# Mixture-of-experts combine: weighted rows added into DRAM by accumulating scatters, instead of a gather and a weighted sum on VectorE

## The reference

```python
flat = rmsnorm(mamba_out + residual, ln_ff_w).reshape(T, D)      # T = 1024 tokens, D = 256
probs = softmax(flat @ router_w.T)                               # 8 experts
topv, topi = top_k(probs, 2)
gate_w = sum(one_hot(topi, 8) * topv[..., None], axis=1)
yexp = einsum('tei,edi->ted', silu(g) * u, w2)                   # g, u: flat through w1, w3 (704 wide)
moe_out = einsum('ted,te->td', yexp, gate_w)
x = layernorm(x + moe_out)
```

## Time and profile before

| | |
|---|---|
| median of 3 runs | 739.64 us (739.38 to 739.97) |
| the profiled execution | 742.04 us, of which the span from first to last instruction is 740.3 us |
| mean granted TensorE clock over the span | 0.914 of full speed |
| PE, weight load, DVE, ACT, POOL busy | 81%, 63%, 65%, 50%, 43% of the span |
| Mamba and routing | 0 to 305 us |
| loop over 21 tiles | 305 to 508 us |

### The profile page before, as it was taken

One profiled execution on the slowest core, in us unless ns is written; L12 is line 12 of the kernel. 1 busy time (PEld: TensorE's weight loads), 2 busy tenths in 40 slices (PEclk: granted clock), 3 DMA queues, 4 the chain that ended last, 5 costly groups with the idle time before them and its releaser, 6 DMA issues.

```text
span 740.3 us, 11054 instructions
## 1 busy us (share of the span) xinstructions
PE 601.6 (81%) x3587; PEld 463.5 (63%) x3587; DVE 480.3 (65%) x751; ACT 371.2 (50%) x819; POOL 321.0 (43%) x255
## 2 busy tenths in 40 slices
PE   2997348787877789899999999899799999945652
PEld 1457147676866677698888888798346555532321
DVE  2686789999899976724444324324544677786995
ACT  4640849999899954522232213115254455323341
POOL 3802038999799996124222442441123222302221
PEclk9997759999999999999999999999999999975555
DMA  6000523111111206504443324115100000000001
GB/s 243 0 29 0 182 80 137 54 58 58 43 58 48 54 15 214 212 31 149 150 148 146 105 78 141 37 29 197 45 0 1 0 0 0 0 0 1 0 0 57
DMA packets 16937, 51.85 MB, mean 70 GB/s; under 512 B 2673, under 2 KB 8562, under 8 KB 15106
## 3 DMA queue, kind: packets, MB, share of 16 engines
q1 hardware_dynamic: 14066, 41.92, 15.8%
q0 software_dynamic: 2688, 7.34, 3.2%
q10 hardware_dynamic: 144, 2.10, 0.7%
HBM read 46.44 MB, written 4.92 MB: 69 GB/s over the span
## 4 chain that ended last, share of the span: by engine, by line
PE 50%; DVE 18%; ACT 12%; POOL 8%; DMA 6%; issue 5%; SPq 1%; DVEq 0%; POOLq 0%; ACTq 0%
PE ps L1545 10%; PE ps L1605 7%; PE ps L1553 7%; POOL arena L381 5%; ACT arena L558 5%; DVE arena L896 5%; PE ps L1280 4%; ACT arena L569 4%; PE ps L1595 4%; DMA moe_out<-arena,result_now 3%; PE ps L1624 3%; PE ps L1402 2%; PE ps L1568 2%; PE ps L1444 2%; DVE x L1215 2%
## 5 line engine op out<-in xcount | busy, mean ns | idle before, releaser
L381 POOL TENSOR_TENSOR arena<-arena 128x1024 f32<-128x1024 f32 x64 | 151.2, 2374 | 19.3 <-DVE arena L896 14.5
L896 DVE TENSOR_TENSOR_SCAN arena<-arena,ps 128x1024 f32<-128x1024 f32 x64 | 146.0, 2285 | 11.3 <-POOL arena L381 7.9
L1545 PEld LDWEIGHTS ps<-arena 128*128 128x128 f32 x924 | 106.1, 192 | 7.8 <-issue 4.2
L1545 PE MATMUL ps<-arena 128*128 128x128 f32 x924 | 107.4, 276 | 3.4 <-DVE arena L1031 2.7
L1359 PE MATMUL ps<-ident,arena 128*128 128x128 f32 x512 | 68.6, 278 | 30.5 <-ACT arena L569 21.3
L558 ACT ACTIVATE arena<-arena,a_neg 128x510 f32<-128x510 f32 x128 | 84.5, 708 | 4.5 <-DVE arena L896 4.4
L569 ACT ACTIVATE arena<-arena,b_tok 128x512 f32<-128x512 f32 x128 | 84.4, 708 | 3.3 <-DVE arena L887 3.3
L1359 PEld LDWEIGHTS ps<-ident,arena 128*128 128x128 f32 x512 | 55.0, 141 | 43.8 <-ACT arena L569 41.8
L657 ACT ACTIVATE arena<-ps 128x256 f32<-128x256 f32 x63 | 24.1, 383 | 111.4 <-PE ps L1545 111.2
L1377 PE MATMUL ps<-ident,arena 128*128 128x128 f32 x512 | 66.5, 273 | 0.5 <-POOL arena L381 0.5
L1553 PE MATMUL ps<-arena 128*128 128x256 f32 x252 | 59.5, 387 | 0.0
(11 more groups left out here) (281 smaller groups left out, 1044.7 us busy)
## 6 DMA issues: line engine op xcount, KB each, us to landing
arena<-in_w_moe SPq DMA_DIRECT2D x8, 2176.0 KB, 8.8
arena<-c_dram SPq DMA_DIRECT2D x32, 256.0 KB, 3.1
arena<-in_w_o ACTq DMA_DIRECT2D x1, 2048.0 KB, 8.5
arena<-in_w_qT SPq DMA_DIRECT2D x1, 2048.0 KB, 11.0
arena<-moe_out SPq DMA_DIRECT2D x4, 512.0 KB, 5.6
arena<-in_w_q SPq DMA_DIRECT2D x1, 2048.0 KB, 12.1
x<-in_x SPq DMA_DIRECT2D x1, 1024.0 KB, 5.8
arena<-in_w_in SPq DMA_DIRECT2D x1, 1024.0 KB, 7.8
```

Source lines behind the costliest of these rows:

```text
L381: pool.tensor_tensor(in_chunks(hC[:, unit % 2, :]), in_chunks(h[:, unit % 2, :]), c_bc[:, m % C_BUFS, :].unsqueeze(1).to_broadcast([P, 2, ...
L896: nc.vector.tensor_tensor_scan(h[:, k, :], dA[:, k, :], ps[:, 2 * k:2 * k + 2, :].rearrange("p a b -> p (a b)"), 0.0, ALU.mult, ALU.add).t ...
L1545: ins = nc.tensor.matmul(ps[:, bank, c * P:(c + 1) * P], w13[:, k, chunk * P:(chunk + 1) * P], xT[:, k, :], start=(k == 0), stop=(k == KD ...
```

## The change

Each result tile is scaled by the weights of its slots as it leaves the matmul output, and the scatter adds it to a table `summed` in DRAM that starts as a copy of x. After the loop the sums are loaded straight into x.

For this, two DRAM-to-DRAM copies fill `summed` at the start (1 MB and 128 KB). The routing gets the row from `row_of` directly, with a row of its own for each unused slot of a tile (`unused`). The weights are brought from tokens to slots by the route that the indices take: each weight is split in three bf16 parts (4 small DVE operations), each part is multiplied into the marks (3 DVE operations on 128 x 416 elements), PE sums the marks with 16 bf16 matmuls 78 columns wide, and DVE adds the three parts to `gate_of_slot` (3 operations). These stand behind `prob` and ahead of the first piece of `quantise` on DVE, and ahead of the loop on PE. The 8 matmuls at L1467, two of the four loads after the loop and the 16 operations at L1052 go.

```diff
+            load(summed[1:1 + T, :], inp["x"].rearrange("b s d -> (b s) d"), "summed_set")
+            load(summed[1 + T:1 + T + P, :], inp["x"].rearrange("b s d -> (b s) d")[0:P, :], "summed_set")
...
-                for k in range(2):
-                    at = 1 + k * T + half * HALF
-                    load(y_got[k][:, half * HALF_TILES:(half + 1) * HALF_TILES, :], moe_out[at:at + HALF, :].rearrange("(i p) d -> p i d", p=P), f"gathered{half}")
+                load(x[:, half * HALF_TILES:(half + 1) * HALF_TILES, :], summed[1 + half * HALF:1 + (half + 1) * HALF, :].rearrange("(i p) d -> p i d", p=P), f"gathered{half}")
...
             pool.wait_ge(s["routed"], 3)
+            pool.wait_ge(s["summed_set"], 32)
...
-                pool.indirect_dma_start(moe_out[:, :], bass.IndirectOffsetOnAxis(result_now[:, 0:1], 0), y_row, None).then_inc(s["y_stored"], 16)
+                pool.indirect_dma_start(summed[:, :], bass.IndirectOffsetOnAxis(result_now[:, 0:1], 0), y_row, None, compute_op=ALU.add).then_inc(s["y_stored"], 16)
                 pool.wait_ge(s["y_stored"], j * 16 + 16)
...
+            nc.vector.tensor_scalar(unused_row[:, :], after_p[:, :], float(T), None, ALU.add)
...
+            link(nc.vector.tensor_scalar(unused[:, :], pos_of[:, :], 0.0, unused_row[:, 0:1], ALU.is_equal, ALU.mult))
             dve.wait_ge(s["routed"], 2)
-            nc.vector.scalar_tensor_tensor(result_of[:, :], index(2), float(T), row_of[:, :], ALU.mult, ALU.add).then_inc(s["routed"], 1)
+            nc.vector.tensor_tensor(result_of[:, :], unused[:, :], row_of[:, :], ALU.add).then_inc(s["routed"], 1)
...
+            chosen = prob[:, :, 0:2].rearrange("p i k -> p k i")
+            link(nc.vector.tensor_copy(gate_part[:, 0, :, :], chosen))
+            link(nc.vector.tensor_tensor(gate_rest[:, :, :], chosen, gate_part[:, 0, :, :], ALU.subtract))
+            link(nc.vector.tensor_copy(gate_part[:, 1, :, :], gate_rest[:, :, :]))
+            link(nc.vector.tensor_tensor(gate_part[:, 2, :, :], gate_rest[:, :, :], gate_part[:, 1, :, :], ALU.subtract))
+            for g in range(3):
+                ins = nc.vector.tensor_tensor(at_gate[:, :, g, :], at_tile[:, :, 2, :],
+                                              gate_part[:, g, :, :].rearrange("p k i -> p (k i)").unsqueeze(2).to_broadcast([P, PICKS, COLS]), ALU.mult)
+            ins.then_inc(s["marked"], 1)
+            dve.wait_ge(s["route_psum"], 4)
+            part = lambda g: ps[:, 6, D + g * COLS:D + (g + 1) * COLS]
+            link(nc.vector.tensor_copy(gate_of_slot[:, :], part(2)))
+            link(nc.vector.tensor_tensor(gate_of_slot[:, :], gate_of_slot[:, :], part(1), ALU.add))
+            link(nc.vector.tensor_tensor(gate_of_slot[:, :], gate_of_slot[:, :], part(0), ALU.add))
...
-                    nc.vector.tensor_copy(y_row, ps[:, 6, 0:D]).then_inc(s["y_ready"], 1)
+                    nc.vector.tensor_scalar(y_row, ps[:, 6, 0:D], gate_of_slot[:, bass.ds(j, 1)], None, ALU.mult).then_inc(s["y_ready"], 1)
...
-                dve.wait_ge(s[f"gathered{half}"], 32)
-                tiles = range(half * 4, half * 4 + 4)
-                for k in range(2):
-                    for n, i in enumerate(tiles):
-                        if k:
-                            dve.wait_ge(s["x1_sum"], half * TILES + n + 1)
-                        nc.vector.scalar_tensor_tensor(x[:, i, :], y_got[k][:, i, :], prob[:, i, k:k + 1], x[:, i, :], ALU.mult, ALU.add).then_inc(s["x1_sum"], 1)
-                for n, i in enumerate(tiles):
-                    dve.wait_ge(s["x1_sum"], half * TILES + n + 5)
+                dve.wait_ge(s[f"gathered{half}"], 16)
+                for i in range(half * HALF_TILES, (half + 1) * HALF_TILES):
                     nc.vector.bn_stats(bn[:, i, :], x[:, i, :]).then_inc(s["bn3"], 1)
...
-            for n in range(TILES, PICKS):
-                ins = nc.tensor.matmul(ps[:, 0, width:width + COLS], at_pos[:, n, :], at_tile[:, n, 2, :],
-                                       start=(n == TILES), stop=(n == PICKS - 1))
...
+            pe.wait_ge(s["marked"], PICKS + 2)
+            for n in range(PICKS):
+                ins = nc.tensor.matmul(ps[:, 6, D:D + 3 * COLS], at_pos[:, n, :], at_gate[:, n, :, :].rearrange("p g m -> p (g m)"),
+                                       start=(n == 0), stop=(n == PICKS - 1))
+            ins.then_inc(s["route_psum"], 1)
```

More of the change, by code:

```diff
@@ L120, in build @@
         at_pos, at_tile = view(104.5, [PICKS, P], BF16), view(108.5, [PICKS, 3, COLS], BF16)
-        y_got = [view(163, [TILES, D]), view(171, [TILES, D])]
+        at_gate, unused = view(111, [PICKS, 3, COLS], BF16), view(114, [COLS])
+        gate_part, gate_rest = view(114.5, [3, 2, TILES], BF16), view(115, [2, TILES])
         w_router = sb("w_router", [P, KD, E])
@@ L150, in build @@
         row_of = sb("row_of", [P, COLS], U32)
+        gate_of_slot = sb("gate_of_slot", [P, COLS])
         result_of = sb("result_of", [P, COLS], U32)
+        unused_row = sb("unused_row", [P, 1])
         pos_of = sb("pos_of", [P, COLS])
@@ L213, in build @@
         hn_rows = nc.dram_tensor("hn_rows", (1 + T, D), F32).ap()
-        moe_out = nc.dram_tensor("moe_out", (1 + 2 * T, D), F32).ap()
+        summed = nc.dram_tensor("summed", (1 + T + P, D), F32).ap()
         ps = ctx.enter_context(nc.psum_tensor("ps", [P, 8, HALF], F32))
@@ L223, in build @@
             routed index_set ld_rows ld_w0 ld_w1 gathered0
-            gathered1 xT_psum xT_done gu_psum gate_act hid_done y_psum y_ready y_stored x1_sum waited
+            gathered1 xT_psum xT_done gu_psum gate_act hid_done y_psum y_ready y_stored summed_set waited
             bn3 eps3 rstd_x1 x1_done ld_v ld_o ld_k ld_qT ld_q kv_psum kv_out k_squared
@@ L1463, in _ @@
                 pe.wait_ge(s["marked"], n + 2)
-                nc.tensor.matmul(ps[:, 0, 0:width], at_pos[:, n, :], at_tile[:, n, 0:2, :].rearrange("p g m -> p (g m)"),
+                ins = nc.tensor.matmul(ps[:, 0, 0:width], at_pos[:, n, :], at_tile[:, n, 0:2, :].rearrange("p g m -> p (g m)"),
                                  start=(n == 0), stop=(n == PICKS - 1))
-            for n in range(TILES, PICKS):
-                ins = nc.tensor.matmul(ps[:, 0, width:width + COLS], at_pos[:, n, :], at_tile[:, n, 2, :],
-                                       start=(n == TILES), stop=(n == PICKS - 1))
             ins.then_inc(s["route_psum"], 1)
```

## The result

The changed kernel takes 751.14 us (median of 4 runs, 749.47 to 753.71), the kernel before 739.81 us beside it (4 runs, 739.38 to 741.16). The ratio is 1.0153 with an interval of 1.012 to 1.0186: slower by 11.3 us, between 8.9 and 13.8. The forecast was 750.5. The profiled execution of the changed kernel takes 751.84 us with a span of 750.1, so 9.8 us more span than before.

What follows compares the result with a forecast made beforehand. PE was taken to set the loop's pace, with DVE's chain bounding the stretch ahead of the first tile. Terms 4.3 + 1.6 + 3.6 + 1.6 - 0.2 = +10.9 us on 739.64 gave 750.5 us, range 743 to 765.

Steps and rivals of the forecast that it cites:

- Weights to slots: On DVE's chain between `prob` and the first tile: added operations and matmuls cost 4.3 us, bounds 3.7 and 5.2.
- The indices: In the routing: two small DVE operations added, L1467 removed; together 0, bounds -0.2 and +0.2 us.
- The clock at the first tile: PE waits some 4.4 us for DVE there, so one lower-clock spell follows: +1.6 us, bounds 0 and 2.
- The scatters: In the loop, beside weight loads: four places where PE needs gathered rows each lose 0.9 us, together 3.6 us.
- d: Extra landing time of an adding scatter, covered in normal tiles: taken as 0.9 us, bounds 0 and 2.9.
- four places: Beside weight loads in the loop: three PE waits for gathered rows and one just in time, each losing 0.9 us.
- The clock in the loop: PE's first two waits for rows grow to about 2.6 us; one lower-clock spell: +1.6 us, bounds 0 and 3.2.
- After the loop: x is normalised over 6 us sooner, but PE's list holds it until 525.59: only -0.2 us.
- the copies at the start: DRAM-to-DRAM copies of 1.15 MB, issued on SP last of the first loads: 0, at most +0.5 us.
- Cheap accumulation: Rival for the loop's scatters: d up to 0.3, total +4.1 to +6.9 us, 743.7 to 746.5; chance 0.22.
- Dear accumulation: Rival for the loop's scatters: d of 1.5 and more, 758 us at d = 2; chance 0.27.
- adding scatters get ahead of the load: Rival: beside weight loads they land sooner, PE's three waits and a clock spell vanish, 736.5 us; chance 0.06.

Runs made afterwards that it cites:

- e1: The changed kernel with scatters that store instead of add: 753.77 us, ratio 1.0056 to the kernel before.
- e5: The kernel before with POOL's order turned, the gather first, then the wait for the previous scatter's landing: 733.56 us, ratio 0.9897.
- e8: e5 with smaller quantisation pieces first and the rest one expert later: 733.93 us, ratio 0.9884 to the kernel before.
- e3: The changed kernel with the next expert's weight load held back until the last tile's scatter has landed: 745.10 us, ratio 0.9939 to the kernel before.
- e2: The kernel before with adding scatters, a table starting as copies of x, and own rows for unused slots: 757.03 us, ratio 1.011.
- e6: The kernel before with the weight load held back until the last tile's scatter has landed: 735.17 us, ratio 0.9880.
- e4: The changed kernel with POOL's order turned, the gather first, then the wait for the previous scatter's landing: 745.27 us, ratio 0.9933 to the kernel before.
- e7: e4 with smaller quantisation pieces first and the rest one expert later: 738.76 us, ratio 0.9958 to the kernel before.
- e9: e4 with a second spreading of the quantisation, keeping its L832 operation away from POOL's product: 736.04 us, ratio 0.9932 to the kernel before.
- e11: e9 with the three scale-row products and ACT's copies put between the 64 products ahead of them: 735.47 us, ratio 0.9917 to the kernel before.
- e12: e10 with the three scale-row products and ACT's copies put between the 64 products ahead of them: 734.03 us, ratio 0.9895 to the kernel before.
- e10: e5 with the second spreading of the quantisation, as in e9: 735.70 us, ratio 0.9888 to the kernel before.

## Why the prediction was right, and where its terms were off

**The direction, the place and the size were right.** PE sets the pace of the loop, the change cost time on DVE's chain ahead of it and at the scatters beside weight loads, and the quiet tiles hid it. The forecast was +10.9 us, the profiles show +9.8, the runs +11.3. The terms did not all hold: against the forecast they came out at -0.9 (weights), -1.6 (clock at the first tile), +1.1 (gathered rows), +0.3 (small waits) and -0.4 us (end). That the sum is off by little over 1 us is in part luck.

**Weights to slots: 4.3 forecast, 3.4 in the profile, 4.2 (2.1 to 6.4) for e1, which has the lower clock and the end in it.** Of the 0.9 less, 0.35 is the chain itself: 3.95 us, mostly because the 16 matmuls took 0.76 us and not the 1.0 that I took between 0.6 and 1.8. The other 0.6 is the earlier start of the chain, and the traces divide it. From the counts of the experts to `pos_of`, across the mark tables of PE, DVE needs 6.77 us before and 6.58 after:

```profile
294.84 0.17 DVE L939 TENSOR_SCALAR count<-count_i 128x8 f32<-128x8 int32 x1
...
301.61 0.18 DVE L961 COPY pos_of<-ps 128x26 f32<-128x26 f32 x1 [0.25 <-PE ps L1467]
```

```profile
294.44 0.17 DVE L943 TENSOR_SCALAR count<-count_i 128x8 f32<-128x8 int32 x1
...
301.02 0.19 DVE L966 COPY pos_of<-ps 128x26 f32<-128x26 f32 x1
```

The 14 profiles fall into the same two groups, 6.77 to 6.79 us in the seven with L1467 and 6.58 to 6.59 in the seven without it. So 0.2 us belong to the step "The indices ... Together 0, bounds -0.2 and +0.2", at the edge of its bounds. The other 0.4 was there before the routing began (294.44 against 294.84). It is no saving of this stretch: counted from there, the first tile's DVE work comes 3.8 us later. e5 and e8 are the same program up to there and ran on one chip, and their profiles differ by 1.5 us at that point (295.92 and 294.46), so 0.4 can't be put down to the change.

**The clock at the first tile: 1.6 forecast, 0 in the profile.** PE's wait there was 3.17 us, not 4.4, since DVE came sooner by 0.9 and PE ended its 32 products 0.3 us later, and the clock stayed up behind it. The step that failed is "An idle time of 4.4 is longer than all of these, so I count one spell": behind this wait none came, nor behind 3.18 us at the same place in e3, while in e2 and e6, behind the shorter waits of 2.78 and 2.81 us there, the 12 products took 2.73 and 2.93 us instead of 1.60. What the forecast hadn't thought of is a slow stretch ahead of the wait. In e1 and e4 the 32 products themselves ran at the lower level, in part or whole, and it cost little, for PE had to wait for DVE afterwards anyway.

**The scatters: d = 0.9 forecast, 1.4 measured; 3.6 us of waits forecast, 4.7 in the profile.** This is the term that was mis-sized, and the rule that it went by ("the scatter lands when the load ends, and d comes behind") did not hold with the measured d: four places at 1.4 would be 5.6 us. The three old waits grew by 0.90, 0.68 and 0.86 us, close to the 0.9 of the forecast, as beside a load the adding delayed the landings by 1.0 us on the mean and not by 1.4. That d was too small and its full charge beside loads too much is a second pair of errors that partly cancel. I had named what was left out: "More descriptors for POOL to write are in neither". These are 0.6 of the 1.4, in POOL's issue, and 96 more packets for each scatter. The remaining 0.8 lies close to the 0.9 that I had for reading the old rows and for a gather's slower rows; how it divides between the two stays open. By the rule of the Trainium skill that was weighed there (Collectives: The Full Stack, "The bandwidth ceiling", twice the read traffic) d would be 0.5 us, and the landings don't agree with that as the whole price: they show 1.4. A fifth wait joined the four (502.60, 0.23 us); no weight load is near it, but POOL's key norm stands between the landing and the gather. The place that had been just in time waited 2.07 us, more than one d: its scatter landed 1.9 us later after its issue than before (9.70 against 7.81 us until POOL went on), beside a load that took 9.9 us instead of 8.3; why that load took longer isn't shown. With d at 1.4 the case stayed inside the forecast's (0.3 to 1.5), near its upper edge, and POOL's pace stayed below PE's.

**The clock in the loop: 1.6 forecast, 1.65 found**, but not in the way forecast. It fell at two waits that had grown (355.98, 424.99) and no longer at the last (484.45), which had grown too. Over the loops of all traces, of the waits of PE over 2 us, those of 2.07, 2.16, 2.21, 2.25, 2.32, 2.47, 2.52, 2.78, 2.79 and 2.81 us were followed by matmuls at the lower level, waits of 2.44, 2.69, 2.74, 2.92, 3.11, 3.17 and 3.18 us were not. And nearly the same two waits of 1.74 and some 1.28 us stand ahead of the 32 products in the changed kernel and in e1, but only e1's were slow (and those of e4 and e7, not those of e3, e9 and e11). The length of a wait doesn't foretell it here; what does stays open.

**After the loop: 0.2 forecast, 0.6 found; the copies at the start: nothing, as forecast.** That x would be ready over 4 us too early was right (5.2 us), and e11 and e12 show it by moving what it waits for. The 0.6 is the pace of the 16 transposes alone, 1.94 us against 2.55.

**The rivals.** Cheap accumulation (a d up to 0.3) is excluded by the median landings of the seven kernels that add, 3.8 to 3.9 us. Dear accumulation was near: 1.5 was its lower bound. That adding scatters get ahead of the load is excluded: beside loads they took 8.2 to 9.4 us in the changed kernel, and none landed before its load. All the same e3 to e6 show that its side of the calculation was sound: once the landings no longer hold up the gathers, these waits are won back, and e5 and e6 are 7.6 and 8.9 us faster than the kernel before (8.4 and 6.7 by the medians).

**The best version** that I ran is the kernel before with the gather first or the load held back, at ratios of 0.988 to 0.990 (e5, e6, e8, e10, e12, whose intervals overlap). The best form of the change is e11 at 0.9917, faster than before as well, and behind e12 by 0.2%, which these runs don't resolve. The change can be repaired, but no run shows it to be worth having: from `prob` to the first product after the loop e11 takes 192.24 us in its profile and e12 188.89, 3.4 us less, and these stand against the 3.2 that e11 wins at the end.

## What to carry to other kernels

Before a store becomes an adding store, find out what waits for its landing and what else is in the queues then: here 1.4 us more per scatter cost nothing in nearly all quiet tiles, and with the lower clock behind the waits over 6 us in the loop, nearly all of it at four places beside a 2.2 MB load. If a gather stands behind a store's landing for no reason of data, turn the order or hold the big load back first; that won some 16 us in the changed kernel, more than the change had cost, and 7.6 to 8.9 us in the kernel before. A shorter stage on an engine that others aren't waiting for gives nothing until the list of the engine that is waited for has been shortened too.

## What the runs showed of the hardware

- **An adding indirect scatter** of 128 rows of 1 KB took 1.6 us of POOL to issue (1.0 without adding), 144 packets (48), and landed 3.9 us after its issue began (2.5); beside 2.2 MB loads the difference was 0.6 to 1.0 us on the mean of six (before and after, e7 and e8, e9 and e10, e11 and e12).
- **A small transfer beside a large one.** Scatters of 128 KB, issued 0.8 to 2.0 us behind the start of a 2.2 MB load from another queue, landed 7.1 to 9.4 us after their issue: the adding ones 0.2 to 0.6 us behind the load's own landing, the plain ones from 0.7 us ahead of it to 0.2 behind. Gathers of 128 KB, issued between loads of 1 and 2 MB, took 7.7 to 9.3 us.
- **VectorE beside GpSimd.** A `tensor_scalar` on 128 x 1536 int32 took 0.95 us alone and 4.64 and 5.20 us beside a GpSimd `tensor_tensor` of 3.5 to 4.0 us, ending 0.8 us after it both times. The Trainium skill (SBUF — State Buffer, "SBUF: two separate sides") says that GpSimd and a VectorE instruction that uses both of its ports (or has two inputs on chip) share one pair of ports, held for the whole instruction by the one that starts first while the other is blocked. No run here shows whether this instruction uses both ports. The lengths agree; the order of starts does not plainly, since DVE's record begins 0.3 to 0.4 us before POOL's.
- **Waits without a cause in the trace.** On the first chip ACT had three waits of 2.22, 1.53 and 1.53 us between four copies at 282 to 290 us, which the trace calls "remote", ahead of the loop and in each of that chip's four profiles. They go with the higher level of all times there (749.66 against 741 us for the same kernel). What they are stays open.
